# Graph attention with edges sorted on one core: local places in 8 bits, three values an edge, the target window in two buffers

## The chip, the cores and the metric

The kernel runs on one core of one Trainium2 chip. The time is the device time of one execution in microseconds (us); lower is better. The engines are PE (TensorE, matrix products), DVE (VectorE), ACT (ScalarE), POOL (GpSimd) and SP (SyncE, which here issues DMAs). PEld is PE's loading of weights. All DMAs of the core share 16 DMA engines.

## The reference

6250 nodes with 96 features, 200,000 edges. Every edge asks its source node for q and its target node for k and v, takes a softmax weight a head over the edges of one source, and adds weighted v to the source. The edges come sorted by target (`dst`), and the result is wanted by source.

```python
q = (embeds[rows] @ qW).reshape(e, HEADS, dh)        # rows = src
k = (embeds[cols] @ kW).reshape(e, HEADS, dh)        # cols = dst, sorted
v = (embeds[cols] @ vW).reshape(e, HEADS, dh)
scores = jnp.clip(jnp.einsum('ehd,ehd->eh', q, k), -10.0, 10.0)
exp_s = jnp.exp(scores)
norms = segment_sum(exp_s, rows, nvar)[rows]
w = exp_s / (norms + 1e-08)
res = segment_sum(w[:, :, None] * v, rows, nvar).reshape(nvar, d)
x = _layernorm(x + (embeds + res), axis=-1)
```

## The kernel before

**Before the sorting (about the first 135 us).** PE projects x to q, k and v. k and v are split in three bf16 parts and go to DRAM as `kv_table`; q stays in SBUF. DVE turns the edge lists into tables of per-edge values in `cols_work`: `src_tile` (which tile of 128 nodes the source is in), `src_tag` (its place in the tile, plus 1), `dst_hi` and `dst_lo` (the target's number in two parts), `dst_local` (the target less the smallest target of its group of 1792 edges) and `inner`. L1293 makes `dst_local`, L1302 and L1304 the two parts, L1308 the tag.

**The sorting (about 135 to 860 us).** The edges are 112 groups of 1792. A lap handles QUAD = 2 groups (u = 0 and 1), so there are 56 laps. A lap works on three stages of different laps at once, which `emit(a, b, c)` names, with b = a - 1 and c = a - 3:

- Stage a finds the place of each edge among the edges of its source tile. DVE compares tiles (`hit`, L1410, into `hits`), PE sums them over the partitions into `slots` in PSUM (L1160, L1162), DVE multiplies the hits by the slots (`mask`, L1477, one instruction a group, second operand in PSUM), adds up (`slot_sums`, L1484), splits the rank in bits (`ranks`, L1490 to L1504), makes a one-hot of the high part (`onej`, L1459), multiplies it by four values an edge (`values`, L1464, four instructions into `vals`) and makes the one-hot of the low part (`parts`, L1470, two instructions).
- Stage b carries the values to their sorted places: PE multiplies `parts` by `vals` (`sort`, L1149, 28 products with 64 columns: four values by 16 columns), and ACT keeps the result (L911, L912). The local places among it are turned by PE (L1138), copied by ACT to `local_rows` (L918), written by SP to DRAM (`sorted_local`, 8 KB, L786) and read back by SP, after that has landed, into all 128 partitions (`brow`, L800): 128 rows of 8192 bytes, 1024 KB in all.
- Stage c makes k and v of every sorted edge. DVE compares `brow` with the partition's number (`pick`, L1438, 2048 f16 elements a group into `picked`) and finds the places of the runs (`stair`, L1441). PE finds destinations (L1113, read by DVE's `place`, L1449) and multiplies `picked` by `window`, the 128 rows of `kv_table` that the group's targets lie in (`kv`, L1131, 48 products with 192 columns a group, in four parts of PSUM). ACT moves each part to `payload` (L903). POOL scatters the payload to DRAM with 4 indirect DMAs a group (L635), after which it can be filled again two laps later.

**What sets the order.** Each engine follows its own program in the order written, and waits on semaphores. `first_phase` (L433) runs the laps. In a lap PE does sort, slots, turn, then kv(0), kv(1); DVE does pick(0), stair(0), pick(1), stair(1), mask, sums, place(0), ranks, values, place(1), parts, hit; ACT does the copies of b, then those of c. `window` has one buffer for each u: SP can load the next lap's window u (L770, 144 KB) only when the last kv(u) of this lap is done (`kv_made[3]`). SP's order in a lap is: local rows out, wait for kv(0), window 0, wait for the local rows' landing, broadcast, wait for kv(1), window 1. PE waits for `window_in[u]` ahead of kv(u).

**After the sorting (865 us to the end)**, the sorted edges are read back in blocks and attention is computed. The program of that part stands unchanged.

## Time and profile before

| | us |
|---|---|
| median of 3 runs (1707.88 to 1710.03) | 1709.44 |
| the profiled execution | 1711.48 |
| its span from first to last instruction | 1709.3 |

| share of the span busy | PE | PEld | DVE | ACT | POOL |
|---|---|---|---|---|---|
| whole span | 87% | 83% | 86% | 74% | 59% |

The span is what the trace covers; the execution's own time is 2.2 us longer, and the median is 2.0 us below that execution. Busy shares are means over stages with different limits, and issue and waiting times don't count as busy. In a timeline row, the number behind `[` is the idle time of that engine just before the row, with what ended it; "issue" means that the profile names no releaser.

### The profile page before, as it was taken

Reading aid. Unit: us, or ns where it says so; the run is one execution under the profiler, and the core shown is the slowest. Engines: PE = TensorE matmul, PEld = TensorE weight load, DVE = VectorE, ACT = ScalarE, POOL = GpSimd, SP = SyncE. Lnnn points to the kernel's source line nnn. Section 1 sums busy time; section 2 is a strip of 40 time slices with the busy share of each in tenths; the row PEclk is TensorE's granted clock in tenths of the full one; section 3 lists DMA queues with packets and bytes.
Section 4 is the critical chain, followed back from the end, with each engine's and each line's share of the span. In section 5 each row is a group of like instructions: output and inputs, shape, how many; then the busy total and the mean of one; then the engine's idle time right before and its main releaser. Section 6 shows DMA issues by size and latency. Waiting matters only on the chain.

```text
span 1709.3 us, 56067 instructions
## 1 busy us (share of the span) xinstructions
PE 1482.0 (87%) x19964; PEld 1425.5 (83%) x19965; DVE 1469.3 (86%) x2980; ACT 1265.3 (74%) x1844; POOL 1016.7 (59%) x764
## 2 busy tenths in 40 slices
PE   4873988888888988888769999999999999999990
PEld 3652878888788878887759999999999999999990
DVE  6988998898988998898158999999999999999987
ACT  2341665565666666665559999999999999999984
POOL 6230776777777776777725555555555555555551
PEclk8566999999999999999979999999999999999995
DMA  5673899999999999999897777777777777777732
GB/s 155 225 276 132 312 370 337 336 346 366 348 352 343 341 367 339 357 339 344 333 302 257 238 238 241 244 238 239 239 243 242 237 240 240 243 239 237 240 113 56
DMA packets 159451, 465.03 MB, mean 272 GB/s; under 512 B 36994, under 2 KB 59266, under 8 KB 152244
## 3 DMA queue, kind: packets, MB, share of 16 engines
q1 hardware_dynamic: 123572, 301.16, 54.1%
q0 software_dynamic: 35840, 163.36, 23.9%
q8 instruction: 23, 0.38, 0.1%
q14 instruction: 16, 0.13, 0.0%
HBM read 271.21 MB, written 209.73 MB: 281 GB/s over the span
## 4 chain that ended last, share of the span: by engine, by line
PE 80%; DVE 8%; issue 6%; DMA 2%; SPq 2%; ACT 1%; POOL 0%; DVEq 0%; POOLq 0%; ACTq 0%
PE two_a L1131 14%; PE two_b L1131 13%; PE meta L1193 12%; PE sum_bank L1193 12%; PE two_a L1214 7%; PE two_b L1214 7%; PE one_d L1204 3%; PE one_c L1204 3%; PE meta L1149 2%; PE one_d L1160 2%; DMA work<-kv_table 1%; PE sum_bank L1113 1%; SPq L825 1%; DVE acc L1614 1%; DVE cols_work L1315 1%
## 5 line engine op out<-in xcount | busy, mean ns | idle before, releaser
L698 POOL TENSOR_TENSOR work<-work 128x768 f32<-128x768 f32 x236 | 450.8, 1910 | 357.4 <-ACT work L939 357.4
L635 POOL DMA_INDIRECT sorted_rows<-work x448 | 501.3, 1119 | 215.2 <-issue 215.2
L948 ACT ACTIVATE work<-work 128x1024 f32<-128x1024 bf16 x236 | 500.8, 2122 | 0.0
L1131 PE MATMUL two_a<-work 128*128 128x192 bf16 x2688 | 268.5, 251 | 86.8 <-issue 84.3
L903 ACT ACTIVATE work<-two_a 128x768 f32<-128x768 f32 x224 | 181.5, 810 | 187.0 <-PE two_a L1131 186.2
L1131 PEld LDWEIGHTS two_a<-work 128*128 128x128 f16 x2688 | 220.0, 100 | 107.5 <-issue 89.0
L1131 PE MATMUL two_b<-work 128*128 128x192 bf16 x2688 | 267.5, 251 | 0.0
L1193 PE MATMUL meta<-work 128*128 128x100 f32 x1888 | 236.1, 278 | 0.8 <-DVE acc L1548 0.8
L1193 PE MATMUL sum_bank<-work 128*128 128x100 f32 x1888 | 235.2, 278 | 0.0
L1579 DVE TENSOR_REDUCE work<-work 128x32 f32<-128x768 f32 x236 | 225.0, 953 | 8.2
L1131 PEld LDWEIGHTS two_b<-work 128*128 128x128 f16 x2688 | 225.9, 100 | 6.8
L1193 PEld LDWEIGHTS meta<-work 128*128 128x128 f32 x1888 | 220.9, 192 | 1.0 <-issue 1.0
L1193 PEld LDWEIGHTS sum_bank<-work 128*128 128x128 f32 x1888 | 220.1, 192 | 0.0
L903 ACT ACTIVATE work<-two_b 128x768 f32<-128x768 f32 x224 | 181.7, 811 | 49.2 <-PE two_b L1131 48.3
L1564 DVE TENSOR_TENSOR work<-work,node_row 128x1024 bf16<-128x1024 bf16 x236 | 162.0, 686 | 24.6 <-ACT work L933 24.6
L1214 PE MATMUL two_a<-q,work 128*128 x2832 | 141.9, 207 | 3.8 <-ACT work L945 3.8
L1214 PE MATMUL two_b<-q,work 128*128 x2832 | 140.7, 207 | 0.0
L1570 DVE TENSOR_TENSOR work<-two_a,work 128x768 f32<-128x768 f32 x118 | 113.0, 957 | 29.2 <-PE two_a L1214 29.2
L1570 DVE TENSOR_TENSOR work<-two_b,work 128x768 f32<-128x768 f32 x118 | 113.0, 957 | 27.0 <-PE two_b L1214 27.0
L1214 PEld LDWEIGHTS two_a<-q,work 128*128 128x128 bf16 x2832 | 130.9, 99 | 4.5 <-issue 4.3
L1214 PEld LDWEIGHTS two_b<-q,work 128*128 128x128 bf16 x2832 | 130.1, 98 | 0.2
L1438 DVE TENSOR_SCALAR work<-work,node_col 128x2048 f16<-128x2048 f16 x112 | 84.1, 751 | 45.6 <-PE two_b L1131 45.3
(229 smaller groups left out, 2211.8 us busy)
## 6 DMA issues: line engine op xcount, KB each, us to landing
work<-sorted_rows SPq DMA_DIRECT2D x472, 392.0 KB, 3.5
work<-sorted_local SPq DMA_DIRECT2D x56, 1024.0 KB
sorted_rows<-pad_rows SPq DMA_DIRECT2D x49, 392.0 KB, 4.5
work<-kv_table SPq DMA_DIRECT2D x112, 144.0 KB
sorted_rows<-work POOLq DMA_INDIRECT x448
kv_table<-work SPq DMA_DIRECT2D x12, 576.0 KB, 3.4
work<-in_x SPq DMA_DIRECT2D x12, 192.0 KB, 3.8
sorted_local<-work SPq DMA_DIRECT2D x56, 8.0 KB
```

Source lines behind the costliest of these rows:

```text
L635: pool.indirect_dma_start(out=rows_dram, out_offset=bass.IndirectOffsetOnAxis(ap=place_now[:, p, u, b:b + 1], axis=0), in_=payload[:, p, u ...
L698: pool.tensor_tensor(now[:, :, 0:D].rearrange("p c (h f) -> p c h f", h=HEADS), blk[:, k, :, :, D:2 * D].rearrange("p m c (h f) -> p (m c) ...
L903: act.activation(payload[:, p, u, KPART * part:KPART * (part + 1), 0:2 * D].rearrange("p (b k) w -> p b k w", b=2), kv_ps[part % 2], ACT.C ...
L948: act.activation(hot_f[:, k % HOTF], hot[:, k % HOTS].rearrange("p n c -> p c n"), ACT.Copy).then_inc(hotf_made[k % PSEM], 1)
L1131: mm = pe.matmul(to, picked[:, u % 2, k * P:(k + 1) * P], window[:, u, :, n, :], start=(n == 0), stop=(n == 2))
L1193: mm = pe.matmul(sums[k % 2][:, m, :], hot_f[:, k % HOTF, m * BLK + c, :], msg[:, k % MSGS, m * BLK + c, :], start=(c == 0), stop=(c == BL ...
L1204: mm = pe.transpose(turned[k % 2][:, c, :], hot[:, k % HOTS, :, c], ident_b[:])
L1214: mm = pe.matmul(q_ps[k % 2][:, m, c, :], hot_T[:, k % 2, m * BLK + c, :], q3[:, bass.ds(tile, 1), i, :].rearrange("p a d -> p (a d)"), st ...
L1438: dve.tensor_scalar(picked[:, u % 2], brow[:, half, u, :].rearrange("p o w -> p (o w)"), node_col[:], None, ALU.is_equal).then_inc(pick_ma ...
L1564: dve.tensor_tensor(hot[:, k % HOTS], tags[:, k, :].unsqueeze(1).to_broadcast([P, P, CH]), node1_row[:], ALU.is_equal).then_inc(hot_made[k ...
L1570: dve.tensor_tensor(qk.rearrange("p (m c) d -> p m c d", m=PAIR), q_ps[k % 2], blk[:, k, :, :, 0:D], ALU.mult).then_inc(qk_made[k % PSEM], 1)
L1579: dve.tensor_reduce(score[:, k], qk.rearrange("p c (h f) -> p (c h) f", h=HEADS), AX.X, ALU.add).then_inc(score_made[k % PSEM], 1)
```

## The change

Four things are changed.

1. **Local places in 8 bits.** `sorted_local`, `local_rows` and `brow` hold unsigned bytes. The DMA to DRAM carries 4 KB and the broadcast 512 KB (128 rows of 4096 bytes). `pick` reads 2048 bytes a group where it read 2048 f16 values, and writes f16 as before.
2. **Three values an edge.** The targets are made local to their group once, ahead of the laps (in place in `dcol_i`), so the low part of the target is the local place, and `dst_local` is gone. The three values lie interleaved (`held`), and `values` is one instruction over 1344 elements where it was four over 448. PE's sort has 48 columns a product. A copy of the groups' bases (`base_f`) is made, and POOL's branch for groups that span over 127 targets adds it back; that branch isn't taken with these inputs.
3. **Slots in 16 bits.** ACT copies `slots` from PSUM to `slots_h` in SBUF as f16, doubled for the pairs of columns (128x200), and `mask` is one instruction over 1400 elements with both operands in SBUF.
4. **`window` with two buffers.** SP asks for both windows of lap c + 1 at the head of its part for lap c, when kv of lap c - 1 is done. PE waits for both at kv(0).

```diff
-    local_dram = nc.dram_tensor("sorted_local", (2, QUAD * NCH, P), F16).ap()
+    local_dram = nc.dram_tensor("sorted_local", (2, QUAD * NCH, P), U8).ap()
...
-        src_tile, src_tag, dst_hi, dst_lo, dst_local, inner = (columns(n) for n in range(6))
+        src_tile, inner = columns(0), columns(5)
+        held = cols_work[:, 1:1 + NV, :].rearrange("p a b -> p (a b)").bitcast(F16).rearrange("p (g v c) -> p g v c", v=NV, c=HC)
+        src_tag, dst_hi, dst_lo = (held[:, :, v, :].rearrange("p (g h) c -> p g h c", h=HB) for v in range(NV))
...
-        window, at = share(at, [QUAD, 2, 3, D], BF16)
+        window, at = share(at, [2, QUAD, 2, 3, D], BF16)
...
+            def windows(los, p):
+                for u in range(QUAD):
+                    sp.dma_start(window[:, p, u].rearrange("p x a b -> p (x a b)"), kv3[bass.ds(los[u], P), :]
+                                 ).then_inc(window_in[p], 16)
...
+                    los, at_c = bases(plus(sp, c, 1)), counts(sp, c, G2, 0)
+                        group_done(sp, kv_made[KPARTS - 1], u, at_c, 1)
+                    windows(los, 1 - p)
...
+                if a is not None:
+                    act.wait_ge(slots_made, plus(act, a, 1))
+                    if not zero(a):
+                        act.wait_ge(masked_made, a)
+                    act.activation(slots_h, slots.unsqueeze(3).to_broadcast([P, QUAD, NB, HC]), ACT.Copy
+                                   ).then_inc(slots_kept, 1)
...
-            link(dve.tensor_tensor(dst_local, dcol_i, base_ps.unsqueeze(2).to_broadcast([P, NG, COLS]),
-                                   ALU.subtract))
+            link(dve.tensor_tensor(dcol_i, dcol_i, base_ps.unsqueeze(2).to_broadcast([P, NG, COLS]), ALU.subtract))
+            link(dve.tensor_copy(base_f[:], base_ps))
...
-                link(dve.tensor_copy(dst_hi, bits))
+                link(dve.tensor_copy(dst_hi, pairs))
...
-                    for v, held in enumerate((src_tag, dst_hi, dst_lo, dst_local)):
-                        dve.tensor_tensor(vals[:, :, v], onej, quad_of(held, a).unsqueeze(2)
-                                          .to_broadcast([P, GH, NCH, HC]), ALU.mult).then_inc(vals_made, 1)
+                    dve.tensor_tensor(vals, onej.unsqueeze(2).to_broadcast([P, GH, NV, NCH, HC]),
+                                      held[:, bass.ds(times(dve, a, GH), GH)].unsqueeze(3)
+                                      .to_broadcast([P, GH, NV, NCH, HC]), ALU.mult).then_inc(vals_made, 1)
...
-                    dve.tensor_tensor(masked[:, HB * u:HB * (u + 1)], hits[:, 0, u],
-                                      slots[:, u, :].unsqueeze(1).unsqueeze(3).to_broadcast([P, HB, NB, HC]),
-                                      ALU.mult).then_inc(masked_made, 1)
+                    dve.tensor_tensor(masked.rearrange("p (u h) t c -> p u h (t c)", u=QUAD),
+                                      hits[:, 0].rearrange("p u h t c -> p u h (t c)"),
+                                      slots_h.rearrange("p u t c -> p u (t c)").unsqueeze(2)
+                                      .to_broadcast([P, QUAD, HB, NB * HC]), ALU.mult).then_inc(masked_made, 1)
```

SP's queue in a lap in the middle of the sorting, before. The first row loads the two bases of the windows; `kv3_made0` and `kv3_made1` tell that the last part of kv(0) and of kv(1) is done.

```order
L499 TENSOR_LOAD base_i
L500 ISA
L786 DMA sorted_local<-work 32x128 [waits local_rows_made]
L770 ISA [waits kv3_made0]
L770 DMA work<-kv_table 128x576
L792 ISA
L800 DMA work<-sorted_local 128x4096 [waits local_out,brow_in,pick_made1]
L770 ISA [waits kv3_made1]
L770 DMA work<-kv_table 128x576
```

The same lap of SP after the change; the waits named are for kv of the lap before, not of this one.

```order
L507 TENSOR_LOAD base_i
L508 ISA
L782 ISA [waits kv3_made0,kv3_made1]
L782 DMA work<-kv_table 128x576
L782 ISA
L782 DMA work<-kv_table 128x576
L800 DMA sorted_local<-work 32x128 [waits local_rows_made]
L804 ISA
L812 DMA work<-sorted_local 128x4096 [waits local_out,brow_in,pick_made1]
```

Both windows have moved to the head of the lap, and the broadcast no longer stands behind a wait for kv(0).

DVE from the one-hot of the high part to the sums of the next lap, before (`one_d` is the PSUM bank that holds the slots):

```order
L1464 TENSOR_TENSOR work<-work,cols_work 128x14x32
L1449 TENSOR_REDUCE work<-sum_bank 128x4 [waits scattered1_1,dest_made1]
L1470 TENSOR_TENSOR work<-work,node_row 128x1792 x2
L1410 TENSOR_TENSOR work<-cols_work,tile_row 128x1400
L1438 TENSOR_SCALAR work<-work,node_col 128x2048 [waits kv3_made0,brow_in]
L1441 TENSOR_SCALAR work<-run_row,run 114x512
L1438 TENSOR_SCALAR work<-work,node_col 128x2048 [waits kv3_made1]
L1441 TENSOR_SCALAR work<-run_row,run 114x512
L1477 TENSOR_TENSOR work<-work,one_d 128x700 [waits slots_made]
L1477 TENSOR_TENSOR work<-work,one_d 128x700
L1484 TENSOR_REDUCE work<-work 128x28 [waits masked_made]
```

And after (L1464 stood four times in a lap before; L1482 stands once):

```order
L1482 TENSOR_TENSOR work<-work,cols_work 128x1344
L1468 TENSOR_REDUCE work<-sum_bank 128x4 [waits scattered1_1,dest_made1]
L1489 TENSOR_TENSOR work<-work,node_row 128x1792 x2
L1429 TENSOR_TENSOR work<-cols_work,tile_row 128x1400
L1457 TENSOR_SCALAR work<-work,node_col 128x2048 [waits kv3_made0,brow_in]
L1460 TENSOR_SCALAR work<-run_row,run 114x512
L1457 TENSOR_SCALAR work<-work,node_col 128x2048 [waits kv3_made1]
L1460 TENSOR_SCALAR work<-run_row,run 114x512
L1495 TENSOR_TENSOR work<-work 128x1400 [waits slots_kept]
L1503 TENSOR_REDUCE work<-work 128x28 [waits masked_made]
```

The order stays; five instructions have become two, and the mask waits for ACT's copy (`slots_kept`) instead of PE's sums. On ACT that copy (L927) stands between the copy of the sorted values and that of the local rows.

## Rows read from the trace of the kernel before

**Rows 1.** Busy time by stretch; engines in turn, then granted clock, DMA share, GB/s.

```profile
340.00:440.00 100.00, 88.76 (x1254) 83.52 (x1251) 91.56 (x203) 63.09 (x111) 74.11 (x66) 0.98 0.97 357
```

**Rows 2.** Timeline, DVE: the compare of tiles, once a lap, in five laps.

```profile
166.97 0.88 DVE L1410 TENSOR_TENSOR work<-cols_work,tile_row 128x1400 f16<-128x1400 f16 x1
...
308.91 0.88 DVE L1410 TENSOR_TENSOR work<-cols_work,tile_row 128x1400 f16<-128x1400 f16 x1
...
323.61 0.88 DVE L1410 TENSOR_TENSOR work<-cols_work,tile_row 128x1400 f16<-128x1400 f16 x1
...
382.80 0.88 DVE L1410 TENSOR_TENSOR work<-cols_work,tile_row 128x1400 f16<-128x1400 f16 x1
...
801.85 0.88 DVE L1410 TENSOR_TENSOR work<-cols_work,tile_row 128x1400 f16<-128x1400 f16 x1
```

**Rows 3.** Timeline, DVE and POOL in one lap: start us, us, engine, what.

```profile
368.85 1.13 POOL L635 DMA_INDIRECT sorted_rows<-work  x1 [0.30 <-issue]
...
369.43 2.08 DVE L1470 TENSOR_TENSOR work<-work,node_row 128x1792 f16<-128x1792 f16 x2
370.28 1.08 POOL L635 DMA_INDIRECT sorted_rows<-work  x1 [0.30 <-issue]
371.43 0.88 DVE L1410 TENSOR_TENSOR work<-cols_work,tile_row 128x1400 f16<-128x1400 f16 x1
371.66 1.50 POOL L635 DMA_INDIRECT sorted_rows<-work  x1 [0.30 <-issue]
372.23 0.75 DVE L1438 TENSOR_SCALAR work<-work,node_col 128x2048 f16<-128x2048 f16 x1
...
373.20 0.73 DVE L1438 TENSOR_SCALAR work<-work,node_col 128x2048 f16<-128x2048 f16 x1
373.46 1.32 POOL L635 DMA_INDIRECT sorted_rows<-work  x1 [0.30 <-issue]
...
374.12 1.66 DVE L1477 TENSOR_TENSOR work<-work,one_d 128x700 f16<-128x700 f16 x2
...
375.08 0.97 POOL L635 DMA_INDIRECT sorted_rows<-work  x1 [0.30 <-issue]
...
375.81 1.61 DVE L1484 TENSOR_REDUCE work<-work 128x28 f32<-128x1400 f16 x1
```

**Rows 4.** Timeline, SP and PE: window 1 issued, and PE's kv(1) that uses it.

```profile
372.55 0.34 SPq L770 DMA_DIRECT2D work<-kv_table  x1
...
380.43 1.15 PE L1131 MATMUL two_a<-work 128*128 128x192 bf16 x12 [1.80 <-issue]
```

**Rows 5.** A long lap: PE's kv(1) after its wait, and that stretch's busy times.

```profile
333.38 2.08 PE L1131 MATMUL two_a<-work 128*128 128x192 bf16 x12 [2.46 <-issue]
...
332.00:336.00 4.00, 2.62 (x17) 2.52 (x18) 4.00 (x8) 0.50 (x1) 3.39 (x3) 0.61 0.89 336
```

**Rows 6.** Groups by line and shape, 300 to 740 us (36 laps): busy, mean ns, idle before.

```profile
L635 POOL DMA_INDIRECT sorted_rows<-work x288 | 325.0, 1128 | 116.4 <-issue 116.4
L1131 PE MATMUL two_a<-work 128*128 128x192 bf16 x1728 | 172.6, 251 | 56.1 <-issue 55.1 <-DMA work<-kv_table 0.9
...
L1477 DVE TENSOR_TENSOR work<-work,one_d 128x700 f16<-128x700 f16 x72 | 60.3, 878 | 12.1 <-PE one_d L1162 11.9
...
L1438 DVE TENSOR_SCALAR work<-work,node_col 128x2048 f16<-128x2048 f16 x72 | 54.1, 752 | 22.1 <-PE two_b L1131 22.0
L1464 DVE TENSOR_TENSOR work<-work,cols_work 128x448 f16<-128x448 f16 x144 | 46.7, 386 | 5.2
...
L912 ACT ACTIVATE work<-meta 128x96 f32 x36 | 9.0, 250 | 0.0
```

**Rows 7.** DMA queues, 300 to 740 us: packets, MB, share of 16 engines.

```profile
q0 software_dynamic: 22958, 105.10, 59.6%
q1 hardware_dynamic: 17253, 48.44, 36.2%
```

**Rows 8.** Groups by line and shape, 60 to 180 us: one table of edges made.

```profile
L1302 DVE CAST cols_work<-work 128x1568 f16<-128x1568 int32 x1 | 1.0, 977 | 0.0
```

More of the change, by code:

```diff
@@ L24 @@
 U32 = mybir.dt.uint32
+U8 = mybir.dt.uint8
 P = 128
@@ L95, in gnn_program @@
     AW = D + HEADS
-    NV = 4
-    TW = (NV - 1) * NCH
+    NV = 3
+    TW = NV * NCH
     TI = FULL_NT // TSLOT
@@ L212, in gnn_program @@
         masked, at = share(at, [GH, NB, HC], F16)
+        slots_h, at = share(at, [QUAD, NB, HC], F16)
         oneh, at = share(at, [GH, P, HC], F16)
@@ L224, in gnn_program @@
         local_v, at = share(at, [P], F16)
-        local_rows, at = share(at, [P], F16)
+        local_rows, at = share(at, [P], U8)
         place_now, at = share(at, [2, QUAD, RB], F32)
@@ L766, in bases @@
                 return words(sp, regs[0:QUAD], base_i, times(sp, c, QUAD), N - 1)
-            def window_of(u, lo, at_c):
-                group_done(sp, kv_made[KPARTS - 1], u, at_c)
-                sp.dma_start(window[:, u].rearrange("p x a b -> p (x a b)"), kv3[bass.ds(lo, P), :]
-                             ).then_inc(window_in[u], 16)
+            def windows(los, p):
+                for u in range(QUAD):
+                    sp.dma_start(window[:, p, u].rearrange("p x a b -> p (x a b)"), kv3[bass.ds(los[u], P), :]
+                                 ).then_inc(window_in[p], 16)
             def emit(a, b, c, p=None):
-                following = c is None or not isinstance(c, int) or c + 1 < NQ
                 if c is None and b == 1:
-                    los = bases(0)
+                    windows(bases(0), 0)
+                if c is not None and (not isinstance(c, int) or c + 1 < NQ):
+                    p = parity(c, p)
+                    los, at_c = bases(plus(sp, c, 1)), counts(sp, c, G2, 0)
                     for u in range(QUAD):
-                        window_of(u, los[u], {})
-                if c is not None and following:
-                    c1 = plus(sp, c, 1)
-                    los, at_c = bases(c1), counts(sp, c, G2, 1)
+                        group_done(sp, kv_made[KPARTS - 1], u, at_c, 1)
+                    sp.sem_inc(sp_turn, 1)
+                    windows(los, 1 - p)
                 if b is not None:
@@ L787, in emit @@
                                  ).then_inc(local_out, 16)
-                if c is not None and following:
-                    window_of(0, los[0], at_c)
                 if b is not None:
@@ L802, in emit @@
                                  ).then_inc(brow_in, 16)
-                if c is not None and following:
-                    for u in range(1, QUAD):
-                        window_of(u, los[u], at_c)
             first_phase(sp, emit)
@@ L1512, in emit @@
                 if a is not None:
-                    for u in range(QUAD):
-                        mask(u)
+                    mask()
                     slot_sums()
```

51 lines of the change are left out of this document (30 added, 21 removed).

## The prediction

> **What bounds the kernel now.** I read the stretches first. In the sorting, nothing is idle for long: from 340 to 440 us DVE is busy 92%, PE 89%, and the DMA engines 97% [rows 1]. So no share alone names the bound, and the lap has to be measured. DVE's compare of tiles stands once in a lap: from 166.97 to 801.85 us there are 52 laps, 12.21 us each [rows 2]. But the laps are not alike. The one that ends at 382.80 began at 371.43 and took 11.37 us [rows 2, 3]; the one from 308.91 to 323.61 took 14.70 [rows 2]. There are a floor and a disturbance, and the change acts on both.
>
> The floor: in the lap of 11.37 us DVE has no idle entry at all. It works from parts to hit, pick, stair, mask and sums without a gap [rows 3]. POOL is as full: an indirect DMA takes 0.97 us and the next starts 0.30 later, 1.27 together, and eight are due in a lap, 10.2 us. Beyond that it is held by DVE. Its issue at 371.66 took 1.50 us; the compare on DVE ran until 372.31, and POOL's ended 0.85 after that. At 370.28 the same with the first one-hot (until 370.51, end at 371.36), at 373.46 with the second pick (until 373.93, end at 374.78). The issue at 375.08 ran beside a mask whose second operand is in PSUM, and took 0.97 [rows 3]. So an issue that starts beside a DVE instruction on 16-bit data wholly in SBUF ends 0.85 us after that instruction, and one beside an instruction with PSUM is free. Over 36 laps POOL's issues average 1.128 us [rows 6]: 8 x (1.128 + 0.30) = 11.4 us. DVE and POOL both stand at the lap's floor. PE doesn't: even there it idles 1.80 us ahead of kv [rows 4].
>
> The disturbance: PE waits 55 us in 36 laps ahead of kv, once in each lap, and the releaser isn't named [rows 6]. SP issued window 1 at 372.55 and kv(1) began at 380.43, after 1.80 us idle [rows 4]: almost 8 us for 144 KB, on DMA engines that are full. SP can't ask earlier, since kv of the lap before reads the only buffer. Where that wait is long it is paid twice: after 2.46 us idle the kv part took 2.08 us instead of 1.15, in a stretch where the granted clock was 0.61 on average [rows 5], so mostly at the lower of PE's two levels, 1.2 and 2.4 GHz. DVE then waits for kv (22 us ahead of the picks) [rows 6], and the lap is 13 to 14.7 us. The mean lap is 0.84 us above the floor by this.
>
> **The change, part by part.**
>
> *Two window buffers.* The issue moves from the end of kv(1) to the head of SP's lap, one lap ahead; kv needs it over a lap (11 us) later, against the 8 us seen. Both waits on windows go, and with them most of the double payment. Worth up to 0.84 us a lap. The broadcast no longer stands behind SP's wait for kv(0); its data is used two laps later, so that moves nothing. SP has no other work that the new wait, for kv of the lap before, could hold up: it is over when SP's lap begins.
>
> *8-bit broadcast.* SP's queue takes 36.2% of 16 engines for 48.44 MB in 440 us [rows 7]; per lap 4.4 us for 1.35 MB, of which the broadcast is 1.05 MB, 3.4 us. Halved, it saves 1.7 us of the 11.7 us of DMA time in a lap (95.8% of 12.21), leaving 10.0. That removes the DMA engines as a bound, and by itself moves no lap that DVE and POOL fill.
>
> *pick on bytes.* Today 2048 f16 elements take 0.752 us [rows 6]. No row has a byte operand. Lower bound: the same 0.75. Upper bound: one element at a time, as the mask (700 in 0.878) and the sums (1400 in 1.611) [rows 3, 6]: 1.047 ns each and 0.145, so 2.29 us. Between them stands a cast from 32 to 16 bits, 1568 in 0.977 us [rows 8], two elements at a time: 2048 x 0.52 ns + 0.16 = 1.23 us. I take 1.23, since that row too has one SBUF source and an element size that doesn't match. Twice a lap: +0.96. The Trainium skill (VectorE: DVE Perf Modes, What auto-detection actually checks) says the four-at-a-time mode wants every tensor in 16 bits, while two at a time asks only for one source in SBUF and even sizes; by that the 0.75 is ruled out and the sum is unchanged.
>
> *One mask.* Two of 0.83 (1.66) become one over 1400 elements, all 16-bit in SBUF, as the compare of tiles with its 0.88 [rows 3]: -0.78. ACT's copy before it is 200 columns; a 96-column one took 0.25 [rows 6], so about 0.35. The slots come while DVE still does pick and stair, which have grown by 0.96, so this is hidden; if it weren't, 0.35 a lap. ACT is busy 63% [rows 1], and behind its wait stands only the copy of local rows, with its 0.1 us delay far from its use.
>
> *One multiplication by three values.* Four take 46.7 / 36 = 1.30 us [rows 6]. From 448 elements in 0.386 and 1400 in 0.878 the slope is 0.517 ns, so 1344 take 0.85: -0.45. PE's 28 products with 48 columns instead of 64 save PE at most 0.3 us, which it has to spare: nothing.
>
> DVE's lap: 11.37 + 0.96 - 0.78 - 0.45 = **11.10 us**.
>
> *What this does to POOL.* The mask now has both operands in SBUF and will hold POOL's issues; the picks hold it longer; the multiplication is one block of 0.85 where there were gaps. I lay DVE's new lap out from the start of parts: one-hots to 1.08 and 2.08, hit 2.00 to 2.88, pick 2.80 to 4.03, stair to 4.32, pick 4.25 to 5.48, stair to 5.74, mask 5.66 to 6.54, sums to 8.15 (free), multiplication 10.26 to 11.11. Now POOL by the rule above, starting 1.15 after each release. Held to 1.08, it starts at 2.23, is held to 2.88, starts at 4.03 (held to 4.32), 5.47 (to 5.74), then 6.89, 8.17, 9.44, 10.72, where the multiplication holds it to 11.11, and next at 12.26. That is 1.16 into the next lap, past the first one-hot and into the second, which holds it to 2.08. From there: 3.23 (pick, to 4.03), 5.18 (pick, to 5.48), 6.63, 7.91, 9.19, 10.46 (to 11.11), 12.26: only seven issues a lap, where eight are due. POOL falls behind, payload isn't free, and DVE waits at place, in the part of its lap that holds nobody. With 0.6 us of waiting there the issue at 10.72 gets in ahead of the multiplication, the next falls into the first one-hot, and eight fit. So the lap settles near **11.7 us**; I take 11.75 for what is left of the disturbance. The Trainium skill (SBUF — State Buffer, Who interferes with whom) states that a Vector instruction with two SBUF inputs contends with a GpSimd instruction that reads SBUF. The issues at 370.28 and 371.66 agree; the page speaks against putting the slots in SBUF.
>
> *Outside the full laps.* The first three laps have no stage c and are DVE's alone: -1.23 each, -3.7. Ahead of the laps three tables are written in runs of two elements instead of in one: between nothing and 0.8 us each (0.977 [rows 8] against one at a time), and there is the copy of the bases: +1.5 in all. Everything after the sorting is untouched.
>
> **The sum.** 52 x (12.21 - 11.75) = 23.9, plus 3.7, less 1.5: 26.1 us. The profiled execution took 1711.5, its span 1709.3; it would become 1685.4, and the median, 2.0 lower, **1683 us**.
>
> **The rivals.**
>
> *DVE alone sets the lap (25%).* POOL's issues fall more kindly than in my layout, as at 375.08 [rows 3]; a shift of 0.2 us decides it. Lap 11.10: 52 x 1.11 + 2.2 = 60 us, 1649.
>
> *POOL slips to seven issues a lap (15%), slower.* The place is the pair pick and mask on DVE. If DVE's waits don't land ahead of the multiplication, eight issues take 8/7 x 11.1 = 12.7 us: 52 x 0.49 - 2.2 = +23 us, 1733. It decides from a mean issue of 1.23 us (8 x 1.53 = 12.2), against 1.128 now [rows 6]. For it: each of the three edits on DVE adds holding time. Against: waits tend to make room.
>
> *Bytes go one at a time (12%), slower.* pick 2.29 us, lap 11.37 + 3.08 - 1.23 = 13.22: +52.5 - 2.2, 1760. It decides from a pick of about 1.8 us. The cast [rows 8] speaks against it.
>
> *The change does nothing (6%).* If the time to land and the long laps come from POOL's own traffic (59.6% of the engines [rows 7]), laps stay at 12.21 and only the first three gain: 1707.
>
> **How the numbers follow.** My forecast, laps of 11.5 to 12.0, has 42%: 1670 to 1697. The range is 1648 to 1733: it takes in the first two rivals and the last, 88%, and leaves the slow byte out. A measurement of this kernel can't tell less than about 0.2% from no change. Faster 0.67 (42 + 25), same 0.06, slower 0.27 (15 + 12).
>
> **What the profile after would show.** pick at 1.23 us and not 0.75 or 2.29; mask 0.88, multiplication 0.85; PE's wait at kv gone or under 10 us in 36 laps, and no stretch of the sorting with a clock near 0.6; DMA share of the sorting at 85 to 90%; POOL's issues with a mean of 1.15 to 1.25 us and hardly any gap over 0.30; laps of 11.5 to 12.0. I am wrong if the laps are over 12.2 with a pick of 1.2, if PE still waits at kv, or if the time outside the sorting moves by over 3 us.

## The result and the profile after

| | us |
|---|---|
| kernel before, median in the same series (1707.88 to 1710.03) | 1709.22 |
| changed kernel, median of 4 runs (1743.52 to 1748.43) | 1746.84 |
| ratio, 95% interval | 1.0218 [1.0201, 1.0236] |
| forecast | 1683 (1648 to 1733) |

The change makes the kernel 37.6 us slower. The forecast has the wrong sign, and the time lies above its range; the rival on the slower side, POOL slipping, had 1733.

First the busy times by stretch, the same stretch as [rows 1], and then the whole middle of the sorting; columns as there: PE, PEld, DVE, ACT, POOL, granted clock, DMA share, GB/s.

```profile
340.00:440.00 100.00, 82.85 (x1142) 77.97 (x1138) 81.33 (x156) 57.16 (x108) 81.41 (x62) 0.95 0.80 286
300.00:740.00 440.00, 366.93 (x5071) 345.95 (x5069) 363.38 (x682) 256.32 (x476) 356.87 (x273) 0.95 0.81 290
```

The DMA engines are relieved (97% before, 80% now), and DVE and PE are less busy than before. Only POOL gained. The groups by line and shape, 300 to 740 us (34 laps), answer to [rows 6]:

```profile
L643 POOL DMA_INDIRECT sorted_rows<-work x273 | 357.6, 1310 | 83.2 <-issue 82.0 <-ACT work L908 1.2
L1149 PE MATMUL two_a<-work 128*128 128x192 bf16 x1637 | 167.2, 255 | 72.2 <-ACT work L912 72.1
...
L1457 DVE TENSOR_SCALAR work<-work,node_col 128x2048 f16<-128x2048 uint8 x68 | 87.7, 1290 | 3.7 <-PE two_b L1149 3.5
...
L1495 DVE TENSOR_TENSOR work<-work 128x1400 f16<-128x1400 f16 x34 | 30.0, 883 | 4.4 <-ACT work L927 3.2 <-issue 1.2
L1482 DVE TENSOR_TENSOR work<-work,cols_work 128x1344 f16<-128x1344 f16 x34 | 29.2, 858 | 5.9 <-DVE work L1478 5.8 <-issue 0.2
L908 ACT ACTIVATE work<-work 128x16 f32 x68 | 15.6, 230 | 88.8 <-DMA sorted_rows<-work 88.8
...
L1468 DVE TENSOR_REDUCE work<-sum_bank 128x4 uint32<-128x12 f32 x68 | 11.2, 164 | 55.1 <-DMA sorted_rows<-work 55.1
```

POOL's issue takes 1.310 us where it took 1.128, and 83 us of idle time over 273 issues is 0.305 each: it never waits for anything else. ACT waits 88.8 us for `payload` and DVE 55.1 us for the places, both released by the scatters (`sorted_rows<-work`), and PE waits for ACT. So everyone waits for POOL, directly or through another engine. Over the 52 laps from 163.57 to 829.57 us the lap is 12.81 us, and 8 x (1.302 + 0.305), with POOL's mean over all 448 issues, is 12.86. The two must agree where an engine never waits, so the formula is no proof by itself; that POOL's gaps are all 0.30 us is.

DMA queues, 300 to 740 us, beside [rows 7]:

```profile
q0 software_dynamic: 21807, 99.81, 58.3%
q1 hardware_dynamic: 16320, 28.00, 22.4%
```

Where the 35.8 us in the sorting come from: the first compare of tiles stands at 133.62 (134.40 before), -0.8; the three laps behind it take 29.95 instead of 32.57, -2.6; 52 laps, +31.1; and from the last compare to POOL's last issue it takes 63.1 instead of 55.1, +8.1, since POOL now ends its laps behind the others (44 issues start behind the last compare, 38 before). The last issue ends at 892.7 instead of 856.9. After it 852.3 us follow, 852.4 before: the rest is untouched.

### The profile page after: what moved, and what is told of

It is laid out like the page before. It is cut to its first block, busy times and chain, and to the rows that moved or that the text cites. A ratio compares the mean times of both kernels' runs of the same rounds, so it can differ in the third digit from the quotient of the medians.

```text
span 1745.0 us, 55834 instructions
## 1 busy us (share of the span) xinstructions
PE 1484.4 (85%) x19964; PEld 1427.7 (82%) x19965; DVE 1459.4 (84%) x2757; ACT 1266.4 (73%) x1900; POOL 1099.9 (63%) x764
## 4 chain that ended last, share of the span: by engine, by line
PE 66%; DMA 14%; DVE 8%; ACT 4%; issue 3%; SPq 2%; POOL 2%; ACTq 0%; DVEq 0%; POOLq 0%
DMA sorted_rows<-work 13%; PE meta L1211 12%; PE sum_bank L1211 12%; PE two_a L1149 10%; PE two_a L1232 7%; PE two_b L1149 7%; PE two_b L1232 7%; PE one_d L1222 3%; PE one_c L1222 3%; ACT work L912 2%; PE meta L1167 2%; PE one_d L1178 2%; POOL sorted_rows L643 1%; SPq L834 1%; DVE acc L1632 1%
## 5 line engine op out<-in xcount | busy, mean ns | idle before, releaser
L643 POOL DMA_INDIRECT sorted_rows<-work x448 | 583.2, 1302 | 170.0 <-issue 167.8
L1149 PE MATMUL two_a<-work 128*128 128x192 bf16 x2688 | 272.7, 254 | 115.3 <-ACT work L912 115.2
L1149 PEld LDWEIGHTS two_b<-work 128*128 128x128 f16 x2688 | 231.9, 101 | 4.6
L1457 DVE TENSOR_SCALAR work<-work,node_col 128x2048 f16<-128x2048 uint8 x112 | 144.2, 1288 | 8.6 <-PE two_b L1149 8.3
L1588 DVE TENSOR_TENSOR work<-two_a,work 128x768 f32<-128x768 f32 x118 | 113.0, 958 | 28.3 <-PE two_a L1232 28.3
```

Source lines behind the costliest of these rows:

```text
L643: pool.indirect_dma_start(out=rows_dram, out_offset=bass.IndirectOffsetOnAxis(ap=place_now[:, p, u, b:b + 1], axis=0), in_=payload[:, p, u ...
L1149: mm = pe.matmul(to, picked[:, u % 2, k * P:(k + 1) * P], window[:, p, u, :, n, :], start=(n == 0), stop=(n == 2))
L1457: dve.tensor_scalar(picked[:, u % 2], brow[:, half, u, :].rearrange("p o w -> p (o w)"), node_col[:], None, ALU.is_equal).then_inc(pick_ma ...
L1588: dve.tensor_tensor(qk.rearrange("p (m c) d -> p m c d", m=PAIR), q_ps[k % 2], blk[:, k, :, :, 0:D], ALU.mult).then_inc(qk_made[k % PSEM], 1)
```

## What holds an issue, read from the trace after

Timeline of the changed kernel, POOL and DVE in part of one lap (start us, us, engine, what):

```profile
414.73 2.08 DVE L1489 TENSOR_TENSOR work<-work,node_row 128x1792 f16<-128x1792 f16 x2
415.87 1.79 POOL L643 DMA_INDIRECT sorted_rows<-work  x1 [0.30 <-issue]
416.73 0.88 DVE L1429 TENSOR_TENSOR work<-cols_work,tile_row 128x1400 f16<-128x1400 f16 x1
417.52 1.28 DVE L1457 TENSOR_SCALAR work<-work,node_col 128x2048 f16<-128x2048 uint8 x1
417.97 2.42 POOL L643 DMA_INDIRECT sorted_rows<-work  x1 [0.30 <-issue]
...
418.98 1.28 DVE L1457 TENSOR_SCALAR work<-work,node_col 128x2048 f16<-128x2048 uint8 x1
...
420.44 0.88 DVE L1495 TENSOR_TENSOR work<-work 128x1400 f16<-128x1400 f16 x1
420.69 1.47 POOL L643 DMA_INDIRECT sorted_rows<-work  x1 [0.30 <-issue]
```

The prediction's rule gives the issue at 415.87 right: the one-hots end at 416.81, the issue 0.85 later at 417.66. It gives the one at 420.69 right too (mask until 421.32, end 422.16: 0.84). But the issue at 417.97 started beside the first pick, which ended at 418.80; by the rule it ends at 419.65. It ended at 420.39, and the second pick, which began at 418.98, ended at 420.26. So it was held **twice**: at its start, and again shortly before its end, until 0.12 us after the pick in progress. At 417.54, where the issue of 415.87 was 0.12 us from its end, the compare of tiles was running and did not hold it.

Two rules then: (1) an issue that starts beside a DVE instruction on SBUF data of 8 or 16 bits ends 0.85 us after it; (2) one that is 0.12 us from its end when a *pick* is running ends 0.12 us after that pick. I laid both over all 448 issues of each trace. Of the time above 0.97 us an issue:

| kernel | above 0.97 in all | by rule 1 | by rule 2 (issues) |
|---|---|---|---|
| before | 66.7 | 63.7 | 2.5 (12) |
| after | 148.6 | 109.1 | 39.4 (69) |

In both kernels what is left is about 1 us or less. The counts by kind of instruction say what each rule turns on. In the trace after, all 153 issues that started well inside a one-hot, the compare, the mask or the multiplication (two inputs in SBUF) were held, and so were the 42 inside a pick; the 59 inside the sums were not, nor before were the 52 inside the mask with its input in PSUM. Near its end an issue was held by a pick in 68 of 70 cases after, and by a two-input instruction in 1 of 133. The stair, which is a `tensor_scalar` too but on 512 elements, did not hold an issue near its end in any of 40 cases before; why is open. Rule 2 was there before, but picks of 0.75 us are hit less often and for less long than picks of 1.29.

The Trainium skill (SBUF — State Buffer, Who interferes with whom) says that a Vector instruction with two SBUF inputs contends with a GpSimd instruction that reads SBUF, and not with one that only writes, and that a copy, cast or `tensor_scalar` in a mode that uses both ports contends with GpSimd. The trace agrees if an issue reads at its start and writes at its end; that reading of the issue is mine and not shown, and the stair does not fit it. The two delays, and which instruction stands beside each hold, are measured. The same section infers that descriptor generation needs the write side alone and so isn't stalled by two-input instructions; the 153 held issues contradict that, and the measurement decides. The prediction let a pick hold an issue at its start only, and left out the hold near the end.

## The experiments

The ratio of a kernel is to the kernel before in the same series, whose median was 1709.6, 1709.4 and 1710.2 us in the three series of this table. "Lap" is the mean of the same 52 laps. The table collects what all of them gave; the texts below take them one by one.

| kernel | time | lap | POOL mean | 8 x (mean + 0.305) |
|---|---|---|---|---|
| before | 1709.2 | 12.21 | 1.119 | 11.39 |
| after | 1746.8 | 12.81 | 1.302 | 12.86 |
| after, an extra sum on DVE | 1740.3 | 12.66 | 1.282 | 12.69 |
| after, mask from PSUM | 1739.4 | 12.60 | 1.279 | 12.67 |
| after, one window buffer | 1735.0 | 12.55 | 1.273 | 12.63 |
| before, with bytes | 1729.7 | 12.35 | 1.248 | 12.42 |
| after, halved picks | 1710.9 | 12.15 | 1.215 | 12.16 |
| after, one window buffer, no bytes | 1705.2 | 12.10 | 1.197 | 12.01 |
| after, one window buffer, halved picks | 1694.5 | 11.87 | 1.185 | 11.92 |
| the last, everything long halved | 1673.7 | 11.53 | 1.131 | 11.49 |
| before, two window buffers | 1729.6 | 12.52 | 1.105 | 11.28 |
| after, 16-bit places, mask from PSUM | 1731.9 | 12.60 | 1.141 | 11.57 |
| before, two buffers, windows last | 1763.7 | 13.07 | 1.098 | 11.22 |
| before, halved | 1709.4 | 12.12 | 1.101 | 11.25 |

In the nine rows from "after" to "everything long halved" the last column gives the lap within 0.1 us. In the other five POOL has gaps and the lap is 0.8 to 1.9 us longer than that; their DMA engines are 92% to 97% busy.

### The windows' part alone, and with three values

The kernel before with two window buffers and SP's new order, nothing else:

```diff
-        window, at = share(at, [QUAD, 2, 3, D], BF16)
+        window, at = share(at, [2, QUAD, 2, 3, D], BF16)
...
+                        group_done(sp, kv_made[KPARTS - 1], u, at_c, 1)
+                    sp.sem_inc(sp_turn, 1)
+                    windows(los, 1 - p)
```

> Only the two window buffers, on the kernel before. Nothing that DVE does changes, so if POOL's holding by DVE is what set the changed kernel's laps (12.81 us, POOL's issues 1.30 us on average), POOL's mean stays at 1.13 us here, PE's wait at kv goes, and the lap falls from 12.21 to 11.4 or 11.5: 52 x 0.75 = 39 us less, about 1670 us. If instead the scatters' own traffic and landing set the laps (the rival 'does nothing'), the DMA share stays at 95% or more, laps stay at 12.2, and the time is 1705 to 1712.

Measured 1729.62, ratio 1.0107 [1.0083, 1.0131]: slower, where the prediction's term promised a gain, and outside both ranges. Timeline of SP, PE and ACT in one lap:

```profile
471.03 1.10 SPq L770 DMA_DIRECT2D work<-kv_table  x2
...
472.32 0.33 SPq L788 DMA_DIRECT2D sorted_local<-work  x1
...
482.40 1.94 PE L1131 MATMUL two_a<-work 128*128 128x192 bf16 x11 [2.57 <-DMA work<-kv_table]
...
483.13 0.27 ACT L915 ACTIVATE work<-meta 32x128 f16<-32x128 f16 x1 [4.79 <-DMA sorted_local<-work]
483.34 0.34 SPq L800 DMA_DIRECT2D work<-sorted_local  x1
```

The local write of 8 KB was asked for at 472.32 and the broadcast that waits for it only at 483.34. From issue to the last landing, the median in the middle of the sorting is 9.6 us for the local write (5.98 before) and 10.1 us for the windows. The windows stand ahead of the small write on full queues; PE's wait stays (51.7 us in 35 laps against [rows 6]) and has only got a name.

The changed kernel with 16-bit places and the mask read from PSUM (two windows and three values are left):

```diff
-        brow, at = share(at, [2, QUAD, NCH * P], U8)
+        brow, at = share(at, [2, QUAD, NCH * P], F16)
...
-                    act.activation(slots_h, slots.unsqueeze(3).to_broadcast([P, QUAD, NB, HC]), ACT.Copy
```

> The changed kernel with places in 16 bits again and the mask read from PSUM again: two window buffers and the one multiplication by three values are left. DVE's lap is 11.37 - 0.45 = 10.9 us. If POOL's holding rules, POOL's mean is 1.13 to 1.17, eight issues take 11.4 to 11.8, and the time is 1665 to 1685. If DVE's own work rules, the lap is 10.9 to 11.1 and the time 1645 to 1655. If neither and the lap stays near 12.8, the cause is in the windows or in the multiplication: 1745.

Measured 1731.92, 1.0121 [1.0097, 1.0145]. None of the three ranges holds it. PE and ACT wait for the same transfers as in the last kernel (PE at kv 51.7 us again), so DVE's shorter multiplication brings nothing where the queues set the lap.

### The bytes alone

The kernel before with `sorted_local`, `local_rows` and `brow` in 8 bits:

```diff
-        brow, at = share(at, [2, QUAD, NCH * P], F16)
+        brow, at = share(at, [2, QUAD, NCH * P], U8)
```

> Only the places in 8 bits, on the kernel before: pick takes 1.29 us instead of 0.75, the broadcast is halved, one window buffer. DVE's lap is 11.37 + 1.08 = 12.4 us. Holding: POOL's mean rises to 1.18 to 1.25 and the lap is 12.4 to 12.7, 1720 to 1735 us, with DVE and POOL both full. If the full DMA engines were what cost the kernel before its 0.84 us a lap, that comes back here: laps at 12.4 at most, 1700 to 1720, and PE's wait at kv shrinks from 55 us in 36 laps.

Measured 1729.69, 1.0112 [1.0088, 1.0136], lap 12.35. The time is in the range that I gave to the holding; the lap, and PE's shrunken wait, are as I said for the full queues, so both act. PE's kv, DVE's pick and the stretch:

```profile
L1132 PE MATMUL two_a<-work 128*128 128x192 bf16 x1695 | 163.6, 246 | 9.1 <-ACT work L904 8.9
L1439 DVE TENSOR_SCALAR work<-work,node_col 128x2048 f16<-128x2048 uint8 x72 | 92.1, 1280 | 0.0
340.00:440.00 100.00, 87.93 (x1209) 78.27 (x1209) 97.00 (x193) 60.50 (x106) 80.79 (x64) 1.00 0.82 299
```

With one window buffer, PE's wait at kv is gone (56.1 us in [rows 6], 9.1 here, and that for ACT): the windows land in 3.2 us instead of 6.6 once the broadcast is half as large. So the disturbance was the full queues, and the bytes take it away, not the second buffer. The price is DVE at 97% and POOL held to a mean of 1.248, which costs more than the shorter wait gives back.

### DVE's work or POOL's pace

The changed kernel with a thrown-away sum of 700 elements on DVE in each lap:

```diff
+                    dve.tensor_reduce(extra.rearrange("p (g c) -> p g c", g=HB), masked[:, 0:HB].rearrange("p g t c -> p g c t"),
+                                      AX.X, ALU.add)
```

> The changed kernel with one more sum on DVE in each lap (700 elements, a reduction, about 0.87 us, which is thrown away): more work for DVE of a kind that holds no POOL issue. If POOL's pace sets the lap, DVE has room for it (it waits about 1.6 us a lap for scatters to land) and the time stays within 8 us of 1747. If DVE's work sets the lap, 56 x 0.87 = 49 us are added: 1795.

Measured 1740.34, 1.0170 [1.0146, 1.0194]: within the 8 us that I gave to POOL's pace. With 0.88 us more work a lap on DVE the kernel is 6.5 us *faster* than the changed one. DVE's work doesn't set the lap; the shift gave POOL a mean of 1.282 instead of 1.302.

### Taking the holds away one at a time

Mask again from PSUM, the rest as changed:

```diff
-                    dve.wait_ge(slots_kept, a1)
+                        dve.wait_ge(slots_made, a1)
...
+                                      slots[:, u, :].unsqueeze(1).unsqueeze(3).to_broadcast([P, HB, NB, HC]),
```

> The changed kernel, but the mask of the slots is again two multiplications that read the slot numbers in 32 bits from PSUM (753 ns each), as before, and ScalarE makes no copy of them. Theory H (GpSimd's issues of indirect transfers set the lap, and they are held while VectorE works on 16-bit data of which both inputs lie in SBUF): the 0.88 us mask no longer holds them, so their mean falls from 1.302 to about 1.25 us and the lap from 12.81 to 12.4-12.5 us, although VectorE has 0.6 us more to do: about 1727. Rival D (VectorE's own work or its chain of waits sets the lap): 0.6 us more in each of 52 laps, about 1775. Rival Q (only the DMA queues and the order of the transfers in them matter): 1742-1750, as the changed kernel.

> The same kernel as in the experiment on the mask read from PSUM, on another chip, since on the chip of that run every kernel, the one before too, was 12-20% longer by stages in which no engine was full. Theory H (the 0.88 us mask on 16-bit data holds GpSimd's issues): mean issue about 1.25 us, lap 12.4-12.5, about 1727. Rival D (VectorE's work or its chain sets the lap): about 1775. Rival Q (only queues and order of transfers matter): 1742-1750.

Measured 1739.38, 1.0174 [1.0157, 1.0191]: 7 us faster than the changed kernel, against 20 expected. POOL's mean fell by 0.023, not 0.05. The direction is the hold theory's, with DVE 0.6 us fuller; rival D is out; the time lies 3 us below rival Q's range, so this run alone hardly tells H from Q. The mask is a small part of the holding.

Each pick in two halves:

```diff
-                    dve.tensor_scalar(picked[:, u % 2], brow[:, half, u, :].rearrange("p o w -> p (o w)"),
-                                      node_col[:], None, ALU.is_equal).then_inc(pick_made[u % GSEM], 1)
+                    for n in range(2):
+                        at = slice(n * NCH * P // 2, (n + 1) * NCH * P // 2)
+                        now = dve.tensor_scalar(picked[:, u % 2, at], brow[:, half, u, at].rearrange("p o w -> p (o w)"),
+                                                node_col[:], None, ALU.is_equal)
+                    now.then_inc(pick_made[u % GSEM], 1)
```

> The changed kernel, but each pick on bytes is made in two halves of 1024 elements (about 0.7 us each instead of one of 1.29). Theory H (an issue of GpSimd that starts beside a pick stays held until the pick ends): the longest issues fall from 2.1-2.4 to about 1.6 us, GpSimd's mean to 1.24-1.27, the lap to 12.4-12.6: 1725-1735. Rival D (VectorE sets the lap): 0.3-0.5 us more in each of 52 laps, 1762-1770. Rival Q: 1742-1750.

> The same kernel as in the experiment on the pick in two halves, on another chip. Theory H: longest issues 1.6 us instead of 2.1-2.4, mean 1.24-1.27, lap 12.4-12.6, 1725-1735. Rival D: 1762-1770. Rival Q: 1742-1750.

Measured 1710.87, 1.0009 [1.0000, 1.0019]. This edit, which only adds work to DVE, takes 36 us off the changed kernel, more than any of the three forecasts. Groups, 300 to 740 us:

```profile
L643 POOL DMA_INDIRECT sorted_rows<-work x288 | 354.1, 1229 | 87.8 <-issue 83.8 <-ACT work L908 4.0
...
L1459 DVE TENSOR_SCALAR work<-work,node_col 128x1024 f16<-128x1024 uint8 x144 | 101.8, 747 | 0.3 <-PE two_b L1149 0.3
```

The second hold fell from 39.4 to 3.9 us over the 448 issues, the first only from 109.1 to 106.2. With almost nothing but the second hold gone, the lap is 12.15 instead of 12.81: this is the failed step of the prediction, measured nearly by itself.

### The place of the windows

The kernel before with two buffers, but SP asks for the windows last in its lap:

```diff
                                  ).then_inc(brow_in, 16)
+                if c is not None and (not isinstance(c, int) or c + 1 < NQ):
+                    for u in range(QUAD):
+                        group_done(sp, kv_made[KPARTS - 1], u, at_c, 1)
+                    windows(los, 1 - p)
```

> The kernel before, places in 16 bits, with two buffers for the windows, as in the first experiment, but SyncE asks for the windows last in its lap, behind the local write and the broadcast, rather than ahead of them. Theory W (what made the first experiment slow is that the four windows stand ahead of the small local write on full DMA engines): the local write lands after about 6 us again (9.6 in the first experiment), SyncE's wait and ScalarE's wait for it shrink, TensorE no longer waits for windows since they have a lap to land, the lap is 11.5-11.9 and the time 1675-1695. Rival F (on DMA engines that are 95% busy any transfer that stands earlier takes from another, and the windows come late whatever their place): lap 12.2-12.6, 1708-1732.

> The same kernel as in the experiment on windows asked for last, on another chip. Theory W: the local write lands after about 6 us, TensorE no longer waits for windows, lap 11.5-11.9, 1675-1695. Rival F (at 95% busy DMA engines the windows come late whatever their place): lap 12.2-12.6, 1708-1732. On the first chip it was 1.4% faster than the kernel before, which speaks for W but is told by laps in which no engine was full.

Measured 1763.66, 1.0323 [1.0301, 1.0344]: both theories fall. The local write did come back, to 4.3 us. But the windows, now asked for behind a broadcast of 1 MB (7.6 us), land 9.0 us after their issue, and that issue is no longer a lap ahead of kv: at 474.81 for a kv that could have begun at 480.7 and began at 484.92.

```profile
474.13 0.34 SPq L796 DMA_DIRECT2D work<-sorted_local  x1
...
474.81 0.89 SPq L770 DMA_DIRECT2D work<-kv_table  x2
...
484.92 1.55 PE L1132 MATMUL two_a<-work 128*128 128x192 bf16 x12 [4.22 <-DMA work<-kv_table]
```

The changed kernel with one buffer a window and SP's order of before:

```diff
-        window, at = share(at, [2, QUAD, 2, 3, D], BF16)
+        window, at = share(at, [QUAD, 2, 3, D], BF16)
```

> The changed kernel with one buffer for each window and SyncE's order of before, so that what is left of the change is the places in 8 bits, the slots in 16 bits and three values. Theory H (GpSimd's issues set the lap, the windows land early with either buffering once the broadcast is half as large): lap 12.7-12.9, 1740-1750. Rival W2 (the windows at the head of SyncE's lap cost time with light DMA engines too): lap 12.3-12.5, about 1725.

> The same kernel as in the experiment on the changed kernel with one buffer a window, on another chip. Theory H: lap 12.7-12.9, 1740-1750. Rival W2 (windows at the head of SyncE's lap cost time with light DMA engines too): lap 12.3-12.5, about 1725.

Measured 1735.00, 1.0162 [1.0139, 1.0186]: 12 us faster than with two buffers, more than H allowed and less than W2. Laps are even here (the middle half about 12.5 to 12.7) and uneven with two buffers (12.3 to 13.6), and the holds by rule 2 are 28.3 us instead of 39.4. That the windows' place shifts POOL against DVE fits; it was not shown by itself.

### Both together, and every long instruction

Halved picks with one window buffer:

> The changed kernel with each pick in two halves and the windows as before (one buffer each, SyncE's old order). Theory H (in every run with light DMA queues the lap is 8 x (GpSimd's mean issue + 0.305 us), and the mean follows from the VectorE instructions that stand beside it): the two edits each lower the mean, to about 1.19, lap 11.9-12.1, 1697-1708. Rival S (the windows' gain of 12 us in the earlier run came from the phase between VectorE and GpSimd, and the half picks have taken it already): lap 12.1-12.2, 1709-1714.

Measured 1694.52, 0.9917 [0.9891, 0.9944], faster than before and 2.5 us better than H's range; rival S falls. The two gains add: 12 and 16 us for the buffer, 36 and 40 for the halves.

Then also the hits, the mask, the multiplication and the one-hots in two parts each; of the one-hots:

```diff
+                    for n in range(2):
+                        at = slice(i * GH // 2 + 4 * n, i * GH // 2 + 4 + 3 * n)
+                        now = dve.tensor_tensor(oneh[:, at], part_h[:, at].unsqueeze(2).to_broadcast([P, 4 - n, P, HC]),
+                                                node_row[:].unsqueeze(1).to_broadcast([P, 4 - n, P, HC]), ALU.is_equal)
```

> As the last, and also the hits, the mask, the multiplication of values and both one-hots in two halves each: no VectorE instruction on 16-bit or 8-bit data is longer than 0.7 us. It costs VectorE some 0.06 us for each cut, 0.3 a lap. Theory H: GpSimd's mean issue falls to 1.08-1.13, its lap to 11.1-11.5; VectorE's own work of 11.1-11.2 a lap comes next, so the lap is 11.4-11.8 and the time 1672-1692, less than both kernels. Rival D (VectorE's work or chain sets the lap): the cuts only cost, 1712-1725. Rival E (the engines take turns for the port at any boundary, so a cut lets GpSimd in and then costs VectorE the same time): lap 12.0-12.2, 1700-1712.

Measured **1673.67**, 0.9797 [0.9773, 0.9821]: 73 us faster than the changed kernel and 36 us faster than the kernel before, the best of those timed here, and in H's range. Groups and stretch:

```profile
L643 POOL DMA_INDIRECT sorted_rows<-work x306 | 348.0, 1137 | 93.3 <-issue 93.3
L1149 PE MATMUL two_a<-work 128*128 128x192 bf16 x1834 | 176.9, 246 | 0.1
...
340.00:440.00 100.00, 89.80 (x1282) 83.68 (x1280) 96.32 (x236) 65.90 (x121) 78.97 (x70) 1.00 0.87 327
```

The second hold is down to 0.4 us, the first to 72.3. DVE (96%) and POOL (no idle time over 0.5 us between issues) are full together again, in laps of 11.53, and the granted clock of this stretch is full, 1.00. Rival E falls: the cuts did not pay the time back to DVE.

### What each part is worth without the holds

The changed kernel without bytes and with one window buffer:

> The changed kernel with 16-bit places and the windows as before: of the change only the slots in 16 bits and the three values are left. VectorE has 10.6-10.8 us of work a lap, GpSimd's mean issue is near before's 1.12-1.15 (lap of 11.4-11.6 by that), the DMA engines are full as before. If VectorE and GpSimd set the lap as in my sum: 11.6-11.8, 1680-1690. If the full DMA queues do (late windows and local writes): 12.1-12.3, 1703-1712.

Measured 1705.16, 0.9976 [0.9961, 0.9991], in the range that I gave to the full queues; my sum's 1680 to 1690 falls. Yet it can't be said that the queues alone set it: POOL's mean is 1.197 instead of 1.119 without any byte, since the mask and the multiplication now hold it too, and the lap by that is 12.01 of the 12.10. PE again waits for windows:

```profile
L1149 PE MATMUL two_a<-work 128*128 128x192 bf16 x1741 | 172.8, 250 | 56.8 <-issue 56.2 <-DMA work<-kv_table 0.5
```

The kernel before with picks, hits and one-hots halved:

> The kernel before with its picks, hits and one-hots each in two halves, nothing else. GpSimd's mean issue falls from 1.119 to 1.04-1.06. Theory H holds for the kernel before only if GpSimd set its lap too: then lap 11.6-11.8, 1680-1690. Rival DQ (the kernel before waits on full DMA queues and on VectorE, which has 0.35 us more to do a lap): 1708-1728.

Measured 1709.42, 1.0003 [0.9990, 1.0017]: POOL's mean fell by 0.018 only, not by 0.06 to 0.08, and nothing moved. So this run hardly took the holds away and can't exclude them. It shows that cutting doesn't always free POOL: 15 issues took over 1.95 us, one of them 4.17, where no issue of the kernel before did, and rules 1 and 2 leave 21 of its 58.7 us unexplained. The longest:

```profile
604.55 4.17 POOL L635 DMA_INDIRECT sorted_rows<-work  x1 [0.30 <-issue]
```

It started 0.08 us into a half one-hot and ended at 608.72, after nine further instructions of 0.3 to 0.7 us that followed each other without a gap; why is open. That the queues cost the kernel before its 0.8 us a lap rests on other rows: in its 52 laps POOL stands idle 40 us beyond its 0.30 between issues, PE's wait at kv is 51 us here and 56 in [rows 6], and with bytes it went.

Two more kernels, the best one with two window buffers and the best one without bytes, were timed only on a chip where every kernel is slower:

> The changed kernel, its two window buffers and SyncE's new order kept, with every long 16-bit or 8-bit VectorE instruction cut in two as in the best version so far. If the windows' part costs by itself (earlier pairs: 12 us more with two buffers at whole picks, 16 us at half picks), 1684-1692, lap 11.7-11.8. If it costs only through the phase between VectorE and GpSimd, which cuts make harmless: 1671-1677, lap 11.4-11.5.

> The best version so far with its local places in 16 bits again: slots in 16 bits, three values, all long instructions cut in two, windows as before. VectorE has 10 us of work a lap, GpSimd's mean issue should fall from 1.197 to 1.08-1.11 (lap 11.1-11.3 by that). If holding was all that was left there: lap 11.2-11.5, 1660-1675, and the bytes were not worth their longer picks. If the DMA engines at 97% busy are the next limit (late windows and local writes, gaps between GpSimd's issues): lap 11.7-12.1, 1688-1705, and the bytes earn their place once the picks are cut.

They gave 2115.6 and 2134.4 with the kernel before at 2015.3. Four earlier kernels had run on another such chip (before 2021.5; mask from PSUM 1960.2, halved picks 2045.4, windows last 1993.6, one window 1933.9). Laps on these two chips take 16 to 20 us, with stretches in which POOL and the DMA engines stand still (DMA share 0.00 from 506 to 510 us with one window) while ACT waits for a release that the profile calls remote; after the sorting they are as fast as the others (850.1 us from POOL's last issue to the end with one window buffer). The order of the kernels is another there: one window is 4% faster than the kernel before and the mask from PSUM 3%, where above they are 1.6% and 1.7% slower, and the two fully cut kernels are 5% and 6% slower. So the causes and gains of this document hold for the chips of the table; what sets the lap on those two is not shown, and what the windows and the bytes are worth once all is cut stays open.

## Why the prediction was wrong

- **Held: the prices on DVE.** Pick 1.290 against 1.23, mask 0.883 against 0.88, multiplication 0.858 against 0.85. The byte operand goes two at a time: 2048 elements in 1.290 and 1024 in 0.747 us, 0.53 ns each. DVE is busy 10.6 us of the 12.81.
- **Held in direction: the queues.** DMA share 80% (85 to 90 was said), PE's wait for windows gone. But PE waits 72 us in 34 laps at kv all the same, now for ACT, and stretches at the lower clock remain, where none near 0.6 was forecast: after 3.38 us of such a wait 12 products took 2.10 us at 712.24, with a granted clock of 0.50.
- **Failed: POOL's walk**, the step "held to 2.88, starts at 4.03". The issue would end at 3.73 beside a pick that runs to 4.03, and is held a second time. The walk had no hold near an issue's end; in the trace 69 issues have one, about 53 of them after a hold at their start. With rule 1 alone the mean would be 0.97 + 109.1 / 448 = 1.214 and the lap 12.15; the second hold adds 0.088 to the mean, 0.70 us a lap. Halving the picks bears this sum out (12.15 measured).
- **Failed: "with 0.6 us of waiting there eight fit", the settling at 11.7.** DVE does wait for places (55 us in 34 laps, 1.6 a lap), but that didn't bring POOL into a kinder place. Once POOL has no gap, the lap is 8 x (mean + 0.305), whatever DVE does. Rule 1 too took more than the settled lap allows: 0.244 us an issue instead of about 0.19 (11.7 / 8 - 0.305 - 0.97), 0.4 us a lap. The rival named the right point, a mean of 1.23; its price of 12.7 us was 0.1 too low, and its 15% far too low: seven issues a lap was what the walk had *found*, and the forecast talked itself out of it. That its price came so near is in part luck: seven issues in 11.1 us are a mean of 1.28, where rule 1 alone gives 1.214 in the trace; the rest came from the hold that the walk left out.
- **Wrong cause: "two window buffers, worth up to 0.84 us a lap".** PE's wait was for full queues. The bytes alone remove it; two buffers alone cost 20 us with full queues and 12 to 16 us with light ones, for a reason that isn't shown in the light case.
- **Outside the laps**: first laps -2.6 against -3.7, tables -0.8 against +1.5, and 8.1 us at the end that had no term, because POOL's backlog has to drain.

## What to carry to other kernels

Where GpSimd issues indirect DMAs beside a busy VectorE, cost each edit on VectorE by how *long* a single instruction is and whether it uses two SBUF inputs or a two-port mode, and not only by the sum of its work; cutting one in two cost 0.06 to 0.12 us here (the picks 1.41 for 1.29, the compare 0.95 for 0.88) and the cuts with the single window buffer brought 73 us. Measure each cut: in the kernel before, cutting brought nothing and made single issues longer. When a walk finds that an engine misses its count in a lap, believe it, and take the count times the mean issue as the lap. A wait on a small transfer is read together with the share of its queues: more buffers don't shorten a transfer that stands in a full queue, less traffic does.

## What the runs showed of the hardware

- An indirect DMA's issue can be held at two points: near its start, ending 0.85 us after a one-hot, compare, mask, multiplication or pick on SBUF data of 8 or 16 bits, and 0.12 us before its end, by a pick in progress (68 of 70 cases), but not by an instruction with two inputs (the compare of tiles at 417.54) and not by the stair. An issue of 0.97 us took up to 2.43 so in the changed kernel and 3.04 with the bytes alone. Behind many short instructions in a row one took 4.17, which these two rules don't give.
- A `tensor_scalar` with a byte input and a 16-bit output runs at 0.53 ns an element, slower than the 16-bit form (2048 in 0.752 [rows 6]) by a factor of 1.7.
- A local write takes 2.4 us to land where the DMA engines are 81% busy (4 KB, the changed kernel), 6.0 at 96% (8 KB, the kernel before), and 9.6 behind 288 KB of windows asked for 1.3 us earlier (8 KB, at 95%).
- After 2.57 us of idle time PE ran 11 products of kv in 1.94 us, where 12 take 1.15, with two window buffers too; the granted clock from 482 to 485 us was 0.50, the lower level of 1.2 GHz. In the changed kernel, where the wait was for ACT, 12 took 2.10 us after 3.38 us idle. So the wait is paid again whether a window or ACT causes it.
